# A two-layer graph kernel: late panels' own units in pairs among others, ring entries in the order they come free, first ring loads behind the first node tiles

## What is computed

```python
# layer 0
A = alpha * adj;  A[i, i] += 1 - alpha
h = relu((A @ x / A.sum(axis=1)[:, None]) @ W.T + b)      # 0 where the sum is 0
x = layernorm(x + h)
# layer 1
xt = logmap0(x)                                            # a factor per row
par = adj   * sigmoid((xt @ w_par[:d])[:, None] + (xt @ w_par[d:])[None, :] + b_par)
chi = adj.T * sigmoid((xt @ w_chi[:d])[:, None] + (xt @ w_chi[d:])[None, :] + b_chi)
x = layernorm(x + proj(expmap0(chi @ xt + par @ xt)))
```

## Time and profile before

| | |
|---|---|
| median of 3 runs | 2229.6 us (2229.26 to 2233.3) |
| the profiled execution, its own time | 2234.23 us |
| its span | 2232.4 us |
| PE / VectorE / ACT / POOL busy | 91% / 87% / 59% / 60% of the span |
| moved by DMA | 818.28 MB, mean 367 GB/s |
| granted TensorE clock, mean | 0.978 |

### The profile page before, as it was taken

The page is one execution under the profiler, slowest core; times in us unless marked ns, Lnnn a source line. Parts: engine busy times, 40 slices in busy tenths (PEclk is TensorE's granted clock), DMA queues, the critical chain, the costliest instruction groups (busy, mean ns, idle before and its releaser), DMA issues.

```text
span 2232.4 us, 18671 instructions
## 1 busy us (share of the span) xinstructions
PE 2035.9 (91%) x5248; PEld 921.2 (41%) x5248; DVE 1938.1 (87%) x1856; ACT 1324.6 (59%) x1508; POOL 1334.0 (60%) x607
## 2 busy tenths in 40 slices
PE   6999999999999999998999977998888888889896
PEld 3444444444434444444444433343344334334433
DVE  5757778988989988898998889998998988989996
ACT  0001324354364454453444578988889989999996
POOL 0000305435455455643633577999998998999996
PEclk9999999999999999999999978999999999999998
DMA  9978988999889988888988998999999999998984
GB/s 342 358 274 297 391 301 359 379 357 373 362 341 405 396 346 356 345 357 324 385 337 340 396 421 318 422 375 420 421 408 385 421 420 381 421 421 342 421 352 190
DMA packets 129222, 818.28 MB, mean 367 GB/s; under 512 B 14928, under 2 KB 27472, under 8 KB 33376
## 3 DMA queue, kind: packets, MB, share of 16 engines
q1 hardware_dynamic: 113104, 792.77, 88.2%
q10 hardware_dynamic: 16016, 24.32, 3.2%
HBM read 808.59 MB, written 8.45 MB: 366 GB/s over the span
## 4 chain that ended last, share of the span: by engine, by line
PE 44%; POOL 17%; issue 11%; DVE 11%; ACT 10%; DMA 5%; ACTq 1%; DVEq 0%; POOLq 0%; SPq 0%
PE ps L1129 28%; POOL chi L541 13%; PE ps L1201 11%; DVE dsum L904 3%; ACT chi L724 3%; DMA ring<-in_g_blk 3%; DVE ps L1002 3%; POOL xA L541 3%; ACT ps L741 2%; DMA ring<-in_a_cols 2%; PE ps L1217 1%; DVE keys L1011 1%; POOL acc L550 1%; ACT L724 1%; ACT xA L724 1%
## 5 line engine op out<-in xcount | busy, mean ns | idle before, releaser
L541 POOL TENSOR_TENSOR chi<-chi,ring 128x1024 f32<-128x1024 f32 x321 | 822.1, 2577 | 668.6 <-ACT chi L724 609.8
L1201 PE MATMUL ps<-keys,xtA 128*128 128x512 f32 x2048 | 978.1, 610 | 130.4 <-DVE keys L1011 96.8
L1129 PE MATMUL ps<-ring,xA 128*128 128x512 f32 x2048 | 922.3, 600 | 45.3 <-DMA ring<-in_g_blk 24.9
L741 ACT ACTIVATE ps<-scores,prcr 128x1024 f32<-128x1024 f32 x472 | 521.8, 1106 | 397.4 <-DVE keys L1011 381.2
L1201 PEld LDWEIGHTS ps<-keys,xtA 128*128 128x128 f32 x2048 | 377.9, 193 | 657.3 <-issue 621.4
L904 DVE TENSOR_TENSOR dsum<-dsum,ring 128x2048 f32<-128x2048 f32 x240 | 592.1, 2467 | 23.6 <-DMA ring<-in_g_blk 16.9
L1129 PEld LDWEIGHTS ps<-ring,xA 128*128 128x128 f32 x2048 | 389.3, 192 | 537.6 <-issue 500.5
L1011 DVE TENSOR_TENSOR keys<-ps,chi 128x1024 f32<-128x1024 f32 x426 | 521.6, 1224 | 81.7 <-issue 28.4
L1002 DVE TENSOR_TENSOR ps<-ps,ring 128x1024 f32<-128x1024 f32 x378 | 462.1, 1223 | 76.1 <-ACT ps L741 72.7
L724 ACT ACTIVATE chi<-scores,prcr 128x1024 f32<-128x1024 f32 x426 | 483.8, 1136 | 16.1 <-DMA scores<-plcl_d 8.9
L541 POOL TENSOR_TENSOR chi<-chi,xA 128x1024 f32<-128x1024 f32 x105 | 247.3, 2376 | 26.2 <-ACT chi L724 26.2
(11 more groups left out here) (111 smaller groups left out, 829.4 us busy)
## 6 DMA issues: line engine op xcount, KB each, us to landing
ring<-in_g_blk SPq DMA_DIRECT2D x460, 1024.0 KB, 9.3
ring<-in_a_cols SPq DMA_DIRECT2D x187, 1024.0 KB, 9.9
xA<-in_a_cols SPq DMA_DIRECT2D x69, 1024.0 KB, 11.1
xA<-in_g_blk SPq DMA_DIRECT2D x32, 1024.0 KB, 12.6
scores<-plcl_d ACTq DMA_DIRECT2D x22, 512.0 KB, 8.1
xA<-in_x_g ACTq DMA_DIRECT2D x64, 64.0 KB, 10.2
yb<-in_xT ACTq DMA_DIRECT2D x8, 512.0 KB, 8.9
x_d<-res ACTq DMA_DIRECT2D x8, 512.0 KB, 9.0
```

The lines of the kernel that those rows point to most:

```text
L541: pool.tensor_tensor(out=chi(n), in0=chi(n), in1=half(t, n), op=ALU.mult).then_inc(m2_ready, 1)
L741: act.activation(dst, scores[:, row, 0, :], ACT.Sigmoid, bias=prcr[:, 2 * jt:2 * jt + 1]).then_inc(p_ready, 1)
L1129: ins = pe.matmul(Y[:, h * BANK:(h + 1) * BANK], xA[:, tile * D:(tile + 1) * D], t[:, tt * BP + h * BANK:tt * BP + (h + 1) * BANK], start= ...
L1201: ins = pe.matmul(outp[:, h * BANK:(h + 1) * BANK], xtA[:, jt * D:(jt + 1) * D], keys(n)[:, h * BANK:(h + 1) * BANK], start=begins, stop=i ...
```

## The change

- `plan`: the eight own units of a panel stand in pairs: two own, two others, and so on, 16 units in all, behind the first 32 others in panel 3 and behind the first 20 in panels 4 to 7. They are now 200 to 213 (200, 201, 204, 205, 208, 209, 212, 213), and likewise from 260, 332, 404 and 468.
- `load_plan`: a panel's four own loads are issued together ahead of its first own unit. From the seventh late load on, the entry taken next is the one whose content is planned to be given back first.
- `APART` leaves out units beside own ones: 28 in place of 37.
- SP waits ahead of ring loads 2 and 4 for the first and the second group of node tiles.
- `natural_of_own` finds the own loads by the new order.

```diff
+OWN_BEHIND_FIRST, OWN_BEHIND = 32, 20
@@ plan
             own = range(p * TPP, (p + 1) * TPP)
             rest = [jt for jt in tiles if jt not in own]
-            tiles = rest + list(own) if p < NPAN - 1 else rest[:24] + list(own) + rest[24:]
+            at = OWN_BEHIND_FIRST if p == EARLY else OWN_BEHIND
+            tiles = rest[:at]
+            for i in range(0, TPP, 2):
+                tiles += [own[i], own[i + 1], rest[at + i], rest[at + i + 1]]
+            tiles += rest[at + TPP:]
@@ load_plan
-        kinds += [("nat", c)] if 2 * c in OWN_AT else [("nat", c), ("trn", c)]
+        if 2 * c not in OWN_AT:
+            kinds += [("nat", c), ("trn", c)]
+        elif OWN_AT[2 * c] % TPP == 0:
+            kinds += [("nat", OWN[OWN_AT[2 * c] + k] // 2) for k in range(0, TPP, 2)]
     entries, held, count, out = list(range(RING)), {}, {}, []
+    def given_back(e):
+        kind, j = held.get(e, ("pair", 0))
+        if kind == "pair":
+            return -1
+        return OWN[OWN_AT[2 * j] // TPP * TPP + TPP - 1] - 2 if 2 * j in OWN_AT else 2 * j + 1
     for i, (kind, j) in enumerate(kinds):
         if i == late + RING - 1:
             entries = list(range(RING, RING + EXTRA)) + entries
-        e = entries.pop(0)
+        e = min(entries, key=given_back) if i >= late + RING - 1 else entries[0]
+        entries.remove(e)
         entries.append(e)
@@
-APART = {n for n in range(MORE + 8, UNITS) if n % 8 == 2 and n not in OWN_AT}
+APART = {n for n in range(MORE + 8, UNITS) if n % 8 == 2 and not {n - 2, n, n + 2} & set(OWN_AT)}
@@ natural_of_own
-            return loaded("nat", (OWN[OWN_AT[n] // TPP * TPP] + k) // 2), k % 2
+            return loaded("nat", OWN[OWN_AT[n] // TPP * TPP + k] // 2), k % 2
@@ sync
+                if kind == "pair" and j in (2, 4):
+                    sp.wait_ge(x_in[j // 2 - 1], 64)
                 wait_free(e, before)
```

## The result

The changed kernel takes **2253.05 us** (median of 4 runs, 2250.91 to 2257.54), the kernel before in the same session 2231.45 (2229.26 to 2235.33). The ratio is 1.0102, 95% interval 1.0087 to 1.0117: slower by 1.0%, some 22 us. Forecast were 2232.7 and a range up to 2244. The profiled execution took 2254.68 us, its span is 2252.8.

A forecast was written before the change was run, and what follows sets the result against it. Bound by the DMA gate of each panel's own loads; three loads (7.5) and hole changes of 4.0 + 2.2 + 2.2 - 0.6 put panel 7's gate at 2108.0, in all +3.1 on 2229.6: 2232.7 us, range 2216 to 2244.

The forecast's parts named there:

- the gate: Landing of a panel's fourth own adjacency load, which the first own unit's transposes need; 185.1 and 185.2 us apart before.
- the hole: Late DMA idle time while SP waits to refill own ring entries; 7.1 us in panel 4 before, 9.3 forecast.
- Rival A: Late panels: DMA stays ahead and engines set the pace, 180.3 us a panel; 2217.3 us, chance 0.23.
- Pairs among others: Own stretches: VectorE sets the pace at 2.40 a unit; 2.2 us per panel of PE-bound time disappear, without reaching the end.
- Four own entries held longer: Panels 4, 5, 6: held 14 units, not 8; release 31.0 us behind the gate, holes +2.2, +2.2, -0.6.
- Rival B: Own stretches: norms on ACT and PE delay the last own turns one unit, each hole 2.40 longer; 2244.7, chance 0.15.
- Panel 3: Its gate moves from 1475.32 to 1415.6; engines are late against the DMA, so its hole is 12.3, before 8.3: +4.0.
- What was left over: Panel 4's period less ring loads and hole, 185.2 - 169.3 - 7.1: 8.8 us of other transfers.
- The sum: Panel 7's gate at 2108.0, unit 511's key at 2212.9 against 2209.81 before: +3.1 us, total 2232.7.
- The start: First ring loads behind the node tiles: 0 at the end, bounds -9.9 and +2.
- Rival C: Start: the third node group lands sooner and PE's long run starts earlier, -4 to -9.9; 2225.7 us, chance 0.12.
- The ring's order: Late ring entries reused in the order they come free: only makes the mixed stretch possible, cost 0.

The follow-up runs named there:

- the hold alone: Kernel before plus one wait: SP refills a panel's own ring entries only after the first product of the unit behind the last own one; 2243.59 us, ratio 1.0053.
- Moving the norms: Changed kernel with the closing steps of panels 0 to 2 hooked 4 units later, behind the last own transposes; 2250.92 us, ratio 1.0083.
- the mixture at the end of the panel: Changed kernel with the own-unit pairs of panels 3 to 6 at places 48 to 61, last panel as in the changed kernel; 2247.41 us, ratio 1.0071.
- the row loads put back: Changed kernel with row loads of groups 22 to 25 hooked at units 273, 345, 345, 417, where the DMA hole lies; 2246.14 us, ratio 1.0073.
- two pairs taken out: Kernel before with row loads of groups 23 and 25 hooked 16 units later, out of the holes of panels 4 and 5; 2233.17 us, ratio 1.0010.
- norms with row loads moved: Changed kernel with closing steps of panels 0 to 2 hooked 4 units later and row loads put back in the hole; 2242.04 us, ratio 1.0059.

## Why the prediction was wrong

**What bounds the kernel** was read rightly: the gate, the hole, one microsecond for one (the hold alone showed it). But the slack on the other side was not seen. With half of the late traffic the kernel before gains only 2 us: a shorter hole could be worth no more, while a longer one costs its full price. Rival A rested on an engines' pace of 180.3 us a panel; halved traffic gave 185.3 before and 185.6 in the changed kernel. By these traces it was not to be had.

**Pairs among others.** Own units do run at 2.40 on VectorE (products of 268 and 269 at 1595.54 and 1597.94). That fewer units in `APART` would not reach the end was right in that nothing was lost, but their worth was not seen: with the old rule, and its 42 units, the time is 12 us higher.

**Four own entries held longer** is the first step that failed, as a size: the release forecast at 31.0 us behind the gate, with a hole of 9.3. Measured were 34.1 to 35.0 and 11.5 to 12.5. In the sum of 31.0 the key that frees the slot ended 30.1 behind the gate and the last transposes followed at once. In the trace two things stood in between.

One is PE's order. When that key ended, PE was in another unit's products, which the norms' 1.8 us had pushed back, and the last transposes began 1.7 us behind it, in panels 4, 5 and 6 alike. Moving the norms took 2.1, 2.5 and 1.4 off the releases. This is Rival B's mechanism, with its 2.40 per hole; I gave it 0.15 on the ground that ACT runs ahead, but it is PE's own order that matters.

The other is the start behind the gate, of which the sum had only the first own unit. The first own product came sooner than taken (0.8 for 1.2 in panel 4), but for the second VectorE waited 1.5, 2.4 and 2.2 us, since its transposes stood behind products at PE's lower clock, and the key ended 1.1, 2.1 and 1.8 us late. No run takes the clock apart from the gate. Moving the norms leaves this part (the release of panel 4 stays 32.0 behind), and the mixture at the end of the panel has it without norms.

The landing erred the other way: 4.8 measured for 5.7 taken. Of the rows of before, those of panels 3 and 4 (6.4 and 5.2) had row loads running beside them; panel 6's 6.5 had none, and what it waited for is open. The Trainium skill's figure (DMA: Bandwidth & Descriptors, Anatomy of one DMA), by which 4.5 came out, stands there for DMAs that GpSimd issues, and these are SP's; it was the nearer one all the same, and the trace has 4.8.

**Panel 3.** Gate 1413.5 for 1415.6; 13.6 for the 12.3 of its hole, though in several pieces, as shown above.

**What was left over** is the second step that failed: "the 8.8 left over in panel 4" was carried into every new period as a constant. Of eight transfers of 512 KB behind panel 4's gate (four of row loads, two of x1, two stores, 1.25 us each) it held about six, for two ran in the hole for almost nothing (the load behind them landed 5.2 us after its issue, not 4.8), because a row load is issued where a group of units ends, and there the hole lay. The change moved the hole away from that place. Three pairs, 7.5 us, with 2.5 of small waits: 10.0. Shown in one direction by the row loads put back (6.5 us of time), and less firmly in the other by two pairs taken out (2.2).

**The sum.** Panel 7's gate was forecast at 2108.0 and came at 2124.9: 9.5 from the holes (49.7 for 40.2), 10.0 from what was left over, less 2.1 for panel 3's earlier gate and 0.5 since panel 5's hole was 7.6 before, not 7.1. That makes the 16.9. The 2.1 is no finding: in the traces of the hold and of the row loads out of the hole, where nothing was changed up to there, panel 3's gate stands 1.9 and 8.6 us sooner than in the trace of before. From panel 7's gate to the last key it took 106.1 us for 104.9 (the terms written down for that stretch add up to 0.2 more than their sum).

**The start** at nothing: right, shown by itself. Rival C did not happen; PE's long run behind the third node group began at 33.53, before at 32.68.

**The ring's order** at nothing holds in the kernel before. In the changed kernel it isn't shown, and the trace speaks against it. The planner takes the four own entries and the two of units 270 and 271 as given back at the same unit, 271, and uses the own ones first. POOL's timeline has the second product of 271, VectorE's the first:

```profile
1598.23 2.36 POOL L566 TENSOR_TENSOR chi<-chi,xA 128x1024 f32<-128x1024 f32 x1
...
1602.73 1.22 DVE L1027 TENSOR_TENSOR ps<-ps,xA 128x1024 f32<-128x1024 f32 x1
```

So one of these entries was free at 1600.6 and the other at 1604.0, while SP stood at an own one until 1608.08. Taken in the other order, the thirteenth load would be the first to wait for `own_turned`; landing at the same 38.9 us behind the gate, it would leave a hole of 38.9 - 13 x 2.49 = 6.5 in place of 11.5, and 7.5 and 7.2 in panels 5 and 6. That is an estimate from this trace; no run tests it.

**Why the range failed.** Rival B had one cause, at 2244.7, and the range ended there. Two causes came together, a later release and the row loads, and the second was in no rival: the remainder was in every case the same number.

No tried version beats the kernel before. Of the changed one the best are the own units in one block and norms with row loads moved, both still 0.6% slower, and with half of the traffic, which is no kernel, the kernel before gains 0.1%.

## What to carry to other kernels

When buffers are held longer, price the release by walking the releasing engine's own order (what stands between its last instructions there, also of other stages), not by the pace of the slowest engine, and check a planned order of reuse for ties against the trace. When an idle stretch of DMA moves, list every transfer that ran in it and ask where each one will run now; a remainder carried over as a constant hides just that. And where two limits are level, a gain in one is worth nothing and a loss its full price: halving one of them in a run shows it at once.

## What the runs showed of the hardware

PE's clock gives way in such a gate. From 1566 to 1574, with PE busy 2.93 of 8 us, the granted clock is 0.77 of full speed in the mean, between its two levels (1.2 and 2.4 GHz). In finer stretches of panel 4 it is near the lower level up to 1578 and back at the upper one behind:

```profile
1570.00:1574.00 4.00, 0.70 (x2) 0.32 (x2) 1.13 (x9) 2.19 (x2) 1.25 (x1) 0.55 1.02 426
1574.00:1578.00 4.00, 3.95 (x10) 2.12 (x11) 2.46 (x2) 0.69 (x1) 1.43 (x1) 0.60 1.01 422
1578.00:1582.00 4.00, 4.00 (x15) 2.09 (x15) 3.22 (x3) 3.19 (x4) 4.00 (x3) 1.00 1.02 420
```

The four products right behind the gate are slow, 3.21 us where four take 1.88 elsewhere:

```profile
1574.05 0.70 PE L1242 MATMUL ps<-ident,ring 128*128 128x128 f32 x2 [1.78 <-DMA ring<-in_a_cols]
1574.55 3.21 PE L1226 MATMUL ps<-keys,xtA 128*128 128x512 f32 x4
```

So a wait of 5 us for DMA costs PE 1.3 us more (1.7 in panel 5), just as it should catch up toward the release. In the kernel before, PE's longest wait for DMA at a gate is 1.3 us.

A load of 1 MB into idle DMA engines lands 4.7 to 4.9 us after its issue, in panels 4 to 7 of the changed kernel and of three experiments (the hold, the norms, norms with row loads); loads one behind the other are 2.49 apart. It isn't always so: with nothing of the kernel's own beside them such loads took 6.5 in panel 6 before and 6.0 in panel 4 with the own units in one block, and the reason is open. With row loads in flight they took 5.2 and 6.4 (one pair) and 9.5 (two pairs).
